# Graph attention on one Trainium2 core: the exponentials of a batch move from SBUF to two PSUM banks

## What is computed

```python
# n = 3125 nodes, H = 4 heads, D = 64; src, dst: 53125 edges sorted by dst
hc = (content @ Wc.T).reshape(n, H, D)
e  = leaky_relu(s[src] + d[dst], 0.2)            # (edges, H)
m  = segment_max(e, dst)
ee = exp(e - m[dst])
a  = ee / segment_sum(ee, dst)[dst]
ft = segment_sum(hc[src] * a[..., None], dst)    # (n, H, D)
h  = ft.reshape(n, H * D) + feat
```

## Time and profile before

| | us |
|---|---|
| median of 3 runs | 3059.55 |
| the runs | 3053.1 to 3060.15 |
| the profiled execution | 3051.82 |
| its span, first to last instruction | 3050.0 |
| POOL busy in the span | 1476.4 (48%) |
| DVE busy in the span | 1600.0 (52%) |
| PE busy in the span | 1400.1 (46%) |
| attention gathers, first start to last end | 1661.9 to 2250.4 |

### The profile page before, as it was taken

One profiled execution on the slowest core, in us unless ns is written; L12 is line 12 of the kernel. 1 busy time (PEld: TensorE's weight loads), 2 busy tenths in 40 slices (PEclk: granted clock), 3 DMA queues, 4 the chain that ended last, 5 costly groups with the idle time before them and its releaser, 6 DMA issues. The chain is left out here.

```text
span 3050.0 us, 30724 instructions
## 1 busy us (share of the span) xinstructions
PE 1400.1 (46%) x7570; PEld 1104.0 (36%) x7570; DVE 1600.0 (52%) x3158; ACT 675.3 (22%) x1519; POOL 1476.4 (48%) x1418
## 2 busy tenths in 40 slices
PE   1647677677849999699983000000004111111104
PEld 0546666566739999355553000000003100000003
DVE  3336565565669999442122566666665134333341
ACT  1111111111237777101021000000002223232231
POOL 0166666666420000330006777777752666676673
PEclk9878888898969999799996555555556555555556
DMA  2356666666235555000003556666542455555563
GB/s 61 128 173 189 191 193 190 187 195 202 67 90 147 152 153 132 0 22 1 1 15 81 184 188 198 190 189 202 184 152 67 138 169 195 175 181 191 166 220 108
DMA packets 274538, 432.05 MB, mean 142 GB/s; under 512 B 108444, under 2 KB 184590, under 8 KB 274476
## 3 DMA queue, kind: packets, MB, share of 16 engines
q1 hardware_dynamic: 208485, 250.96, 25.3%
q0 software_dynamic: 65328, 179.11, 21.7%
q10 hardware_dynamic: 662, 1.28, 0.1%
HBM read 302.15 MB, written 128.80 MB: 141 GB/s over the span
## 5 line engine op out<-in xcount | busy, mean ns | idle before, releaser
L623 POOL DMA_INDIRECT msg_rows<-message_source_table,msg_index x416 | 401.9, 966 | 300.5 <-issue 183.5
L1639 POOL DMA_INDIRECT att_rows<-att_table,lane_source x416 | 462.1, 1111 | 126.7 <-issue 126.7
L1952 POOL DMA_INDIRECT best_rows<-message_source_table,lane_source x416 | 408.5, 982 | 227.0 <-issue 126.2
L2060 DVE SCALAR_TENSOR_TENSOR best_state<-best_state,lane_line,best_rows 128x256 f32<-128x256 f32 x416 | 202.0, 486 | 364.0 <-issue 207.9
L751 PE MATMUL msg_ps_sum<-msg_by_edge,msg_rows 128*128 128x128 f32 x1664 | 256.4, 317 | 174.4 <-DVE aggT L683 114.2
L751 PEld LDWEIGHTS msg_ps_sum<-msg_by_edge,msg_rows 128*128 128x128 f32 x1664 | 241.4, 227 | 201.1 <-issue 185.3
L1671 PE MATMUL att_ps_upto<-ident,att_largest 128*4 128x128 f32 x1 | 0.4, 372 | 617.9 <-DVE att_largest L1727 617.9
L683 DVE TENSOR_TENSOR aggT<-aggT,msg_ps_sum 128x256 f32 x416 | 172.8, 415 | 201.5 <-remote 109.2
L1974 ACT ACTIVATE best_rows<-best_rows,lane_weight 128x256 f32<-128x256 f32 x416 | 177.6, 496 | 430.3 <-DMA best_rows<-message_source_table,lane_source 416.6
L2009 PE MATMUL best_ps_self<-w_selfT,hT 128*125 128x256 f32 x100 | 51.7, 671 | 471.7 <-DVE x L2070 244.4
L735 PE MATMUL msg_ps_window<-msg_window,msg_by_node 128*128 128x256 f32 x832 | 225.9, 413 | 48.8 <-issue 25.0
(11 more groups left out here) (269 smaller groups left out, 2636.8 us busy)
## 6 DMA issues: line engine op xcount, KB each, us to landing
att_states<-aggT SPq DMA_DIRECT2D x104, 528.0 KB
msg_window<-message_window_table SPq DMA_DIRECT2D x416, 128.0 KB
best_states<-best_state SPq DMA_DIRECT2D x104, 512.0 KB
attr_rows<-in_edge_attr SPq DMA_DIRECT2D x103, 192.0 KB, 3.4
msg_line<-place_line SPq DMA_DIRECT2D x52, 256.0 KB
attr_line<-mask_line SPq DMA_DIRECT2D x52, 256.0 KB
attr_carry<-carry_line SPq DMA_DIRECT2D x52, 256.0 KB
msg_rows<-message_source_table,msg_index POOLq DMA_INDIRECT x416
```

Source lines behind the costliest of these rows:

```text
L623: nc.gpsimd.indirect_dma_start(rows[:, s, t, :], None, table, bass.IndirectOffsetOnAxis(ap=index[:, s, t:t + 1], axis=0)).then_inc(self.ro ...
L1639: nc.gpsimd.indirect_dma_start(rows[:, t % ring, :], None, self.attention_table, bass.IndirectOffsetOnAxis(ap=self.lane_source[:, t:t + 1] ...
L1952: nc.gpsimd.indirect_dma_start(rows[:, g % SLOTS, t, :], None, table, bass.IndirectOffsetOnAxis(ap=self.lane_source[:, g * TG + t:g * TG + ...
L2060: nc.vector.scalar_tensor_tensor(out=state[:, s % STATE_BUFS, t, :], in0=before, scalar=self.lane_line[:, bass.ds(at, 1)], in1=rows[:, s, ...
```

## The change

ScalarE's `Exp` writes to PSUM: `att_exps` in SBUF is gone, and two PSUM tensors of a bank each, `att_ps_exps0` and `att_ps_exps1`, are used in turn by batch number. The weighing products and the carrying product read their second operand there. No instruction is added, removed or moved on any engine, and every wait stays as it was. The stage then uses all eight PSUM banks. The line numbers of the pass shift by four.

```diff
-            logit, largest, common, exps = (self.sb(f"att_{k}", [P, 2, H * (BATCH + 1)], ctx=ctx) for k in (
-                "logit", "largest", "common", "exps"))
+            logit, largest, common = (self.sb(f"att_{k}", [P, 2, H * (BATCH + 1)], ctx=ctx) for k in (
+                "logit", "largest", "common"))
...
+            ps_exps = [self.ps(f"att_ps_exps{k}", [P, H * (BATCH + 1)], ctx) for k in range(2)]
...
+            def exps(k):
+                return ps_exps[k % 2][:, 0:H * (BATCHES[k][1] + 1)]
...
-                        nc.scalar.activation(flat(exps, k), flat(logit, k), ACT.Exp).then_inc(exps_made, 1)
+                        nc.scalar.activation(exps(k), flat(logit, k), ACT.Exp).then_inc(exps_made, 1)
...
                         nc.vector.tensor_tensor(
-                            of, of, of_batch(exps, k)[:, :, at:at + TG].rearrange("p h t -> p t h").unsqueeze(3)
+                            of, of, heads(exps(k))[:, :, at:at + TG].rearrange("p h t -> p t h").unsqueeze(3)
                             .to_broadcast([P, TG, H, HS]), ALU.mult).then_inc(moved, 1)
...
                             nc.vector.tensor_tensor(
                                 heads(carried[:]), heads(state[:, (t0 - 1) % held, 0:H * HS]),
-                                of_batch(exps, k)[:, :, 0:1].to_broadcast([P, H, HS]), ALU.mult).then_inc(moved, 1)
+                                heads(exps(k))[:, :, 0:1].to_broadcast([P, H, HS]), ALU.mult).then_inc(moved, 1)
```

## The result

| | before | after |
|---|---|---|
| median, us | 3056.8 | 3087.03 |
| the runs, us | 3053.1 to 3060.15 (4) | 3082.85 to 3867.44 (4) |
| profiled execution, us | 3051.82 | 3089.76 |
| attention pass, first gather to last step, us | 602.2 | 630.4 |

After to before is 1.0092 with a 95% interval of 1.0072 to 1.0113: **slower by 0.9%**, where 1.6% faster was forecast. The longest run, 3867.44, is a slow one and is left out of the ratio.

A forecast was written before the change was run, and what follows sets the result against it. POOL's gathers were taken to bound the attention pass: 65.0 us of stretching less 16 that stays gives 49 us. That made 3002.8 from the profiled run or 3010.5 from the median; forecast 3007 us, range 2991 to 3025.

The forecast's parts named there:

- The rest: Attention pass: POOL needs 20.7 us a batch and remains the bound, with 5.2 us of idle time left on VectorE.
- rival (C): Weighing products: repeated PSUM operand read slowly, VectorE becomes the bound; 3137 us at three times the length; 3%.
- What stretches a gather: Attention pass: VectorE reading two SBUF operands stretches POOL's gathers, not VectorE being busy; 65.0 us of stretching in 25 batches.
- Rival (B): Attention pass: second SBUF operand is not the cause, products still stretch gathers; no gain, 3051.8 to 3059.6 us; 4%.
- Stretching that stays: Attention pass: the 416 steps keep two SBUF inputs and still stretch gathers, 16 us over 25 batches.
- The gain of the mechanism: Attention pass: less stretching lets the last batch of 16 start 49 us earlier, which is the stage's gain.
- The product's length: Weighing product on VectorE: no change from 1234 ns with one operand in PSUM.
- ScalarE's write: `Exp` writing to PSUM: taken as nothing; bound of half of 0.259 us each, 0.5 us either way.
- Rival (A): Attention gathers: DMA transfers capped at 200 GB/s, gain only 26.5 us, time about 3029 us; 6%.
- (D): Attention steps stretch gathers less or more than 16 us: gain 65.0 or 33 us; width of the main case.
- main case: Whole kernel: gain of 43 to 56 us, time 2996 to 3017 us with 3007 between; 87%.

The follow-up runs named there:

- e13: Changed kernel with three 0.6 us GpSimd pauses in each batch and GpSimd at most two batches ahead of VectorE; ratio 1.0014, pass 605.4 us.
- e3: Changed kernel with three 0.6 us GpSimd pauses in each batch; 3073.88 us, ratio 0.9981.
- e1: Changed kernel, but VectorE copies the exponentials from PSUM to SBUF once a batch and the products read the copy; 3085.33 us, ratio 1.002.
- e18: Changed kernel, unedited, measured again in a sitting where the kernel before took 2848.23 us; 2797.02 us, ratio 0.9818.
- e14: Changed kernel with two GpSimd pauses in each batch and GpSimd at most two batches ahead of VectorE; ratio 1.0019, pass 606.5 us.
- e2: Kernel before, with weighing products of 4 values instead of 1040 and no PSUM use in them; 3086.35 us, ratio 1.0029.
- e12: Changed kernel with all 104 state writes to HBM issued behind the attention pass; 3226.74 us (one run), pass 609.9 us.
- e4: Changed kernel with states written 16 tiles at a time, 26 transfers instead of 104; 3089.23 us, ratio 1.0037.
- e11: Changed kernel with GpSimd at most two batches ahead of VectorE instead of three; 3087.72 us, ratio 1.0034.
- e16: Changed kernel with gathers of 64 rows instead of 128; 2792.51 us (one run), where the kernel before took 2848.23 us.
- e17: Changed kernel with gathers of half a row, 134 of 268 values; 2810.4 us (one run), where the kernel before took 2848.23 us.

## Why the prediction was wrong, point by point

**Where it failed.** The step is the one under "The rest": VectorE works 15.5 us in a batch, so POOL at 20.7 "remains the bound, with 5.2 us of idle time left on VectorE". The 15.5 were taken as a property of VectorE's instructions. They hold for fast batches, 15.4 measured after. But in condition A, with a period of 20.4 us, two in five take 30 to 40. VectorE becomes the bound, which was rival (C)'s outcome, by a mechanism that none of the rivals had: the products stay at 1228 ns, and what is late is the seeing of increments between the steps. The arithmetic is above: 163 us less of waiting, 191 more of VectorE's own time.

**The sign was in the rows.** The earlier trace rows stood there for their 982 ns and showed more: in front of L2060 there are 207.9 us of "issue" idle time, more than half of the 361.6 for which these steps stood idle, and POOL waits there 60.4 us for those steps. That stage has unstretched gathers and a step for each tile, which is what the change was to make of the attention pass. After it, the attention pass shows nearly the same figure: 59.4 us of POOL waiting for steps. The waits behind that idle time last up to 1395 ns with a median of 46:

```profile
L2060 DVEq FUSED_REGOPS  x384: 1/46/1395, 2386.2 to 2956.1; - x192
...
  issue: 207.9, 209
```

I took the stage for a model of the gather's duration and did not ask why its steps, 486 ns each and with a steady supply, were idle so long. Read fully, it gave a rival on the slower side; its price could have been estimated. The series suggests that the stretched gathers had kept the attention pass just on the quiet side: its 22.6 us a batch are 0.2 and 0.3 above those of e13 and e3, where the first slow batches appear.

**What held.**

- *What stretches a gather.* The second SBUF operand does: 946 ns (at most 949) inside a product with a PSUM operand, mean 1127 as soon as it is read from SBUF again (e1). Rival (B) is refuted. The Trainium skill ("SBUF — State Buffer", "Who interferes with whom") has `tensor_tensor` not stalling transfers, and infers a reason for it; these runs show that with two SBUF inputs it does stall a gather that GpSimd issues (mean 1127 against 968), and the measurement decides.
- *Stretching that stays.* Forecast 16 us; in e18 it is 410.2 - 416 x 0.946 = 16.7.
- *The gain of the mechanism.* Forecast 49 us; the medians in condition B differ by 51.2. The pass loses 602.2 - 553.9 = 48.3 between the trace of before, which is from A, and e18, which is from B; no trace of the kernel before was taken in B. In e18 VectorE's wait for rows is 140.9 (some 140), POOL's idle only 0.3 each, and VectorE's idle time (140.9 - 15.5) / 24 = 5.2 us in a batch (5.2).
- *The product's length.* Forecast no change from 1234: 1228 and 1229. The fixed part of 120 cycles with a PSUM source that the Trainium skill gives ("VectorE: DVE Perf Modes", the section on the TRN2 errata) does not show; the product got 6 ns shorter, where an estimate from that page has 65 more.
- *ScalarE's write.* Within the bound of half of 0.259 us: `Exp` takes 231 ns, 28 less.
- *Rival (A).* No cap at 200 GB/s: fast stretches after move 241 GB/s at a share of 0.75. *Rival (C)* as stated, a slow PSUM operand, is refuted by the 1228 ns. *(D)* was of the right width.

**The size of the error.** Forecast 3007, range to 3025, measured 3087. The gathers got as short as forecast, but the pass ended 28 us longer instead of 49 shorter: 77 us, put down to the slow stretches. The range was too narrow by the same omission: its main case kept VectorE's pace. The last gather was to end near 2200 and ends at 2255. In condition B a forecast of 49 us less, made from its own before, would have been right within 3 us.

**What is shown and what stays open.** Shown, for the attention pass in condition A: slow stretches come with closely following gathers (e3, e13, e14 against the changed kernel); they need neither PSUM (e2) nor the state writes (e12) nor many of their increments (e4); and they end while the gathers pause (e11 and the timeline). Not shown: what holds the updates or their records to one each 0.70 us, whether the profiler's recording has a part in it, what sets the machine's condition, and whether it is the gathers' requests, their bytes or POOL's instructions that load it (e16 and e17 fell into condition B). Closely following gathers are not the whole story either. In the message stage no wait in front of VectorE's L683 lasts over 53 ns, but 37 waits of SyncE last 698 ns, and the changed kernel takes 109 us longer there in A. Its gathers lie 1.53 us apart on average in A and 1.27 in e18: there the wider spacing comes from being slowed, and does not protect it.

## What to carry to other kernels

Before speeding up the engine that sets the pace, ask whether its neighbours' times were measured at that pace, and look for a stage of the same program that already runs at it. Idle time of "issue" before short instructions that wait for each other, or waits far above their median, is a sign of a resource near its limit, even where the engine is not the bound. Before giving such waits to the chip, count the semaphore updates that the trace recorded against those that the program makes: here they fell short in every trace with such waits. To free a GpSimd gather from a VectorE instruction beside it, one of the two SBUF inputs can go to PSUM, here at no cost in length (1228 ns against 1234); whether the time follows has to be measured on the machine as it is, more than once.

## What was not expected of the hardware

- A gather that starts at least 0.1 us into a VectorE instruction with two SBUF inputs, and 0.13 us before its end, ends 0.82 us after that instruction does (0.815 to 0.830 in 96 cases beside products and 25 beside steps of the kernel before). With one input in PSUM it takes 0.946 us, the same as alone.
- Waits for semaphores can end on a grid of 0.70 us for tens of microseconds, and so do the trace's records of updates. Instructions of 0.49 us that each wait for the one before then start 1.40 us apart instead of 0.52. In the attention pass it was seen only with GpSimd's gathers at 22.4 us or less for sixteen; it was seen in the maximum stage of both kernels too, and only in one condition of the machine, in which the traces have about half of the updates or less.
- That condition cost the kernel before 230 us (2847 to 3077 on one chip). The changed kernel's traces show where it lost 294: 109 in the message stage, 77 in the attention pass, 66 in the maximum stage.
- A gather of 64 rows holds POOL for 897 ns where nothing stretches it, one of 128 for 945.
